# Two 64x64 levels of a block inverse in one matmul group, for two neighbouring chains of a gated delta rule

## The reference

```python
def step(S, x):
    qt, kt, vt, bt, gt = x
    S = S * jnp.exp(gt)[..., None, None]
    kv = jnp.einsum('bhk,ebhkv->ebhv', kt, S)
    delta = (vt[None] - kv) * bt[..., None]
    S = S + kt[None, :, :, :, None] * delta[..., None, :]
    ot = jnp.einsum('bhk,ebhkv->ebhv', qt * scale, S)
    return (S, ot)
```

## Time and profile before

| | |
|---|---|
| median of 3 runs | 3258.17 us |
| lowest and highest | 3254.01 and 3269.35 us |
| span of the profiled execution, which is its own time as the profile has it | 3278.8 us |
| mean granted TensorE clock | 0.943 |
| busy: PE, DVE, ACT, POOL | 91%, 51%, 34%, 45% of the span |
| last link of the chain of waits: PE, issue, DVE, ACT, POOL | 74%, 10%, 6%, 4%, 4% |
| the delta stage | about 1336 to 2008 us of the span |

### The profile page before, as it was taken

The page is one execution under the profiler, slowest core; times in us unless marked ns, Lnnn a source line. Parts: engine busy times, 40 slices in busy tenths (PEclk is TensorE's granted clock), DMA queues, the critical chain, the costliest instruction groups (busy, mean ns, idle before and its releaser), DMA issues.

```text
span 3278.8 us, 46022 instructions
## 1 busy us (share of the span) xinstructions
PE 2990.0 (91%) x16081; PEld 1719.2 (52%) x16081; DVE 1674.9 (51%) x3820; ACT 1128.2 (34%) x2501; POOL 1485.6 (45%) x1471
## 2 busy tenths in 40 slices
PE   7999999888999899679999998998999999999828
PEld 3434566577676544357777765444533333444414
DVE  7633266588244432258777632442257777621361
ACT  3312422297122222345666332221034444332201
POOL 0565656498554457333333103554656666300003
PEclk9999999999999899859999778999999999999958
DMA  5400001210111244334554435211167666600404
GB/s 169 138 19 6 13 19 54 68 43 14 42 51 43 69 159 158 125 97 123 135 132 124 123 112 162 83 52 49 30 203 201 205 198 198 160 13 26 175 4 129
DMA packets 275960, 321.36 MB, mean 98 GB/s; under 512 B 155807, under 2 KB 193569, under 8 KB 275732
## 3 DMA queue, kind: packets, MB, share of 16 engines
q1 hardware_dynamic: 219684, 182.57, 18.7%
q0 software_dynamic: 51840, 134.60, 13.6%
q10 hardware_dynamic: 4208, 1.25, 0.2%
HBM read 215.75 MB, written 104.60 MB: 98 GB/s over the span
## 4 chain that ended last, share of the span: by engine, by line
PE 74%; issue 10%; DVE 6%; ACT 4%; POOL 4%; DMA 1%; SPq 0%; ACTq 0%; DVEq 0%; POOLq 0%
PE bank L2700 8%; PE bank L1522 5%; PE bank L2692 5%; PE bank L708 4%; PE bank L1301 3%; PE bank L2363 3%; PE bank L2854 3%; PE bank L2847 3%; PE bank L439 3%; PE bank L731 2%; PE bank L762 2%; PE bank L1117 2%; PE bank L2343 2%; PE bank L1311 2%; PE bank L858 2%
## 5 line engine op out<-in xcount | busy, mean ns | idle before, releaser
L2672 POOL DMA_INDIRECT conv_src<-xn_rows,keep x288 | 272.4, 946 | 176.4 <-DVE conv_msg L2738 111.4
L291 POOL DMA_INDIRECT sorted_bias<-perf_rec,place x256 | 260.2, 1016 | 145.4 <-PE bank L708 90.1
L2700 PE MATMUL bank<-conv_msg,conv_hot 128*128 128x512 f32 x576 | 273.0, 596 | 0.6 <-ACT conv_msg L2719 0.6
L1923 POOL TENSOR_TENSOR delta_dec<-delta_dec,rates_of 128x512 f32<-128x512 f32 x64 | 67.3, 1051 | 338.4 <-ACT delta_dec L1975 338.4
L2738 DVE TENSOR_TENSOR conv_msg<-bank,conv_src 128x512 f32<-128x512 f32 x288 | 185.5, 686 | 47.3 <-PE bank L2692 47.3
L666 POOL DMA_INDIRECT sorted_edge<-rec,place x128 | 127.2, 994 | 141.0 <-PE bank L1362 75.1
L2719 ACT ACTIVATE conv_msg<-conv_msg 128x1024 f32<-128x1024 f32 x144 | 152.0, 1055 | 102.0 <-DVE conv_msg L2738 102.0
L1117 PE MATMUL bank<-bias_prod,bias_hot 128*128 128x256 f32 x640 | 148.2, 387 | 25.2 <-ACT bias_hot L1070 13.1
L2692 PE MATMUL bank<-conv_we,conv_eT 64*128 64x512 f32 x576 | 164.5, 648 | 0.7 <-ACT conv_eT L2716 0.7
L1101 POOL TENSOR_TENSOR bias_prod<-bias_col,bias_rec 128x512 f32<-128x512 f32 x128 | 147.2, 1179 | 16.5 <-PE bank L1117 15.7
L1117 PEld LDWEIGHTS bank<-bias_prod,bias_hot 128*128 128x128 f32 x640 | 120.1, 192 | 53.8 <-issue 28.2
(11 more groups left out here) (502 smaller groups left out, 6756.2 us busy)
## 6 DMA issues: line engine op xcount, KB each, us to landing
keep<-slot_qkv SPq DMA_DIRECT2D x32, 512.0 KB, 3.9
delta_kv<-slot_qkv SPq DMA_DIRECT2D x32, 512.0 KB, 3.9
sorted_edge<-sort_pad SPq DMA_DIRECT2D x8, 1440.0 KB, 7.3
keep<-sorted_edge SPq DMA_DIRECT2D x18, 640.0 KB, 5.2
slot_out<-delta_o SPq DMA_DIRECT2D x64, 128.0 KB, 2.0
conv_src<-xn_rows,keep POOLq DMA_INDIRECT x288, 3.6
X<-in_x SPq DMA_DIRECT2D x4, 1024.0 KB, 10.9
sorted_bias<-perf_rec,place POOLq DMA_INDIRECT x256
```

The lines of the kernel that those rows point to most:

```text
L291: POOL.indirect_dma_start(out=sorted_bias, out_offset=bass.IndirectOffsetOnAxis(ap=place[:, 0, c:c + 1], axis=0), in_=rec0[:, c, :], in_of ...
L2672: POOL.indirect_dma_start(out=src[:, n % 4, j, :], out_offset=None, in_=xn_rows, in_offset=bass.IndirectOffsetOnAxis(ap=rec[:, g % 3, k + ...
L2700: a = PE.matmul(bank[n % 2][:, :], hot[:, g % 2, k + j, :], msg[:, q, j, :], start=j == 0, stop=j == 1)
```

## The change

- The two steps Zb and T become one step, "Zb and T". For chain n it issues, head by head in turn, the Zb matmul of chain n and the T matmul of chain n - 1. One more such step, for n = NC, holds the last chain's T. It waits for U_ready of n, Zb_ready of n - 1 and T_ready of n - 2.
- `MID` goes from 16.2 to 15.8, and the fractions are set anew: Z .70, Z copy .80, U .05, U copy .15, Zb and T .21, Zb copy .25, T copy .26 (of the chain before), turn .65, kq .75, gram .22.
- Z waits for Z_ready of the chain before in place of T_ready, and U waits for U_ready of the chain before as well: each step waits for the readers of its own region of bank 3.

PE's order in a period is then: U .05, through .20, Zb and T .21, gram .22, decay .25, solve .55, turn .65, Z .70, sums .80. ACT's is: low mask .08, U copy .15, Zb copy .25, T copy .26, (L copy .33), exp .35, w .70, kq .75, Z copy .80.

```diff
--- before.py
+++ after.py
@@ -1701,7 +1701,7 @@
             BT = 4
             NBT = ST // BT
             NC = 2 * ST
-            MID, MAIN = 16.2, 17.2
+            MID, MAIN = 15.8, 17.2
             ALONE = 13
             gt = rates_of
             eg = sb("eg", [P, 3, ST, H])
@@ -1773,14 +1773,15 @@
 
             plan = []
             for n in range(NC):
-                for what, at in (("mask", -0.45), ("turn", -0.2), ("kq", -0.1), ("low mask", 0.08), ("gram", 0.21), ("decay", 0.25),
+                for what, at in (("mask", -0.45), ("turn", -0.35), ("kq", -0.25), ("low mask", 0.08), ("gram", 0.22), ("decay", 0.25),
                                  ("exp", 0.35), ("weigh", 0.45), ("BA", 0.72),
-                                 ("Z", MID + 0.005), ("Z copy", MID + 0.1), ("U", MID + 0.25), ("U copy", MID + 0.35),
-                                 ("Zb", MID + 0.5), ("Zb copy", MID + 0.6), ("T", MID + 0.75), ("T copy", MID + 0.85),
+                                 ("Z", MID - 0.1), ("Z copy", MID), ("U", MID + 0.25), ("U copy", MID + 0.35),
+                                 ("Zb and T", MID + 0.41), ("Zb copy", MID + 0.45), ("T copy", MID + 1.46),
                                  ("kd", MAIN - 0.3), ("through", MAIN), ("r", MAIN + 0.15), ("solve", MAIN + 0.35),
                                  ("w", MAIN + 0.5), ("sums", MAIN + 0.6), ("state", MAIN + 0.75), ("o", MAIN + 0.85),
                                  ("store", MAIN + 1.0)):
                     plan.append((n + at, what, n))
+            plan.append((NC + MID + 0.41, "Zb and T", NC))
             for t in range(ST):
                 plan.append((2 * t - 3.0, "load qk", t))
                 plan.append((2 * t + 1.8, "B out", t))
@@ -2014,7 +2015,30 @@
                                       stop=c == KC - 1)
                         if c == KC - 1:
                             a.then_inc(*gate_done.up())
-                    if what not in ("turn", "decay", "gram", "Z", "U", "Zb", "T", "through", "solve", "sums"):
+                    if what not in ("turn", "decay", "gram", "Z", "U", "Zb and T", "through", "solve", "sums"):
+                        continue
+                    if what == "Zb and T":
+                        if n < NC:
+                            PE.wait_ge(*U_ready.at(n + 1))
+                        if n >= 1:
+                            PE.wait_ge(*Zb_ready.at(n))
+                        if n >= 2:
+                            PE.wait_ge(*T_ready.at(n - 1))
+                        for i in range(HG):
+                            if n < NC:
+                                t, g, hs, MA, MB = places(n)
+                                h = g * HG + i
+                                a = PE.matmul(bank[3][64:128, 256 + 64 * i:320 + 64 * i], BA[0:64, t % R, h, 0, 64:128],
+                                              Lf[0:64, t % 2, h, :], start=True, stop=True)
+                                if i == HG - 1:
+                                    a.then_inc(*Zb_done.up())
+                            if n >= 1:
+                                t, g, hs, MA, MB = places(n - 1)
+                                h = g * HG + i
+                                a = PE.matmul(bank[3][0:64, 256 + 64 * i:320 + 64 * i], Zb[64:128, (n - 1) % 2, i, :],
+                                              U[64:128, t % 2, h, 64:128], start=True, stop=True)
+                                if i == HG - 1:
+                                    a.then_inc(*T_done.up())
                         continue
                     t, g, hs, MA, MB = places(n)
                     r, at = t % R, t % 2
@@ -2056,7 +2080,7 @@
                     if what == "Z":
                         PE.wait_ge(*ul_in[at].at(16 * 7 * (t // 2 + 1)))
                         if n >= 1:
-                            PE.wait_ge(*T_ready.at(n))
+                            PE.wait_ge(*Z_ready.at(n))
                         for i, h in enumerate(heads):
                             PE.matmul(bank[3][32:64, 32 * i:32 * i + 32], BA[0:32, r, h, 0, 32:64], Lf[0:32, at, h, 0:32],
                                       start=True, stop=True)
@@ -2065,6 +2089,8 @@
                         a.then_inc(*Z_done.up())
                     if what == "U":
                         PE.wait_ge(*Z_ready.at(n + 1))
+                        if n >= 1:
+                            PE.wait_ge(*U_ready.at(n))
                         for i, h in enumerate(heads):
                             PE.matmul(bank[3][0:32, 32 * i:32 * i + 32], Zs[32:64, n % 2, i, :], U[32:64, at, h, 32:64],
                                       start=True, stop=True)
@@ -2073,18 +2099,6 @@
                             a = PE.matmul(bank[3][32:64, P + 32 * i:P + 32 * i + 32], U[32:64, at, h, 32:64],
                                           Zs[32:64, n % 2, i, :], start=True, stop=True)
                         a.then_inc(*U_done.up())
-                    if what == "Zb":
-                        PE.wait_ge(*U_ready.at(n + 1))
-                        for i, h in enumerate(heads):
-                            a = PE.matmul(bank[3][64:128, 256 + 64 * i:320 + 64 * i], BA[0:64, r, h, 0, 64:128],
-                                          Lf[0:64, at, h, :], start=True, stop=True)
-                        a.then_inc(*Zb_done.up())
-                    if what == "T":
-                        PE.wait_ge(*Zb_ready.at(n + 1))
-                        for i, h in enumerate(heads):
-                            a = PE.matmul(bank[3][0:64, 256 + 64 * i:320 + 64 * i], Zb[64:128, n % 2, i, :],
-                                          U[64:128, at, h, 64:128], start=True, stop=True)
-                        a.then_inc(*T_done.up())
                     if what == "through":
                         if t >= 1:
                             PE.wait_ge(*state_new.at(n - 1))
```

## The result

The changed kernel takes 3248.56 us (median of 20 runs, 3238.56 to 3255.05), the kernel before 3258.68 us in the same session (20 runs, 3251.54 to 3280.86). The ratio is 0.9956 with a 95% interval of 0.9941 to 0.9972: 0.44% less, some 14 us (the two medians are 10 us apart), where 18 us were forecast. It was repeated twice beside other kernels: 0.9965 (0.9939 to 0.9991) and 0.9934 (0.9909 to 0.9959).

What follows compares the result with a forecast made beforehand. PE bounds one half of each batch, DVE the other. Five batches -10.3, load waits +2.1, last L copy period -1.15, tail -8.5, fill 0: -18 us, from 3258.17 to 3240 us, range 3220 to 3264.

Steps and rivals of the forecast that it cites:

- Part 1: Zb and T merged on PE: 16 alternating records take 0.60 us, saving 0.60 us of PE per chain.
- Part 2: PE-bound half: ACT's loop through the U copies sets a 7.49 us period against 7.79, gaining 0.30 per period.
- Part 3: Period with the L copy, once a batch: through of the next chain comes 1.15 us earlier.
- Part 4: First Z of a batch waits 0 to 0.9 us for loaded blocks, average 0.35; +2.1 us in all.
- Part 5: DVE-bound half of each batch: DVE's list is unchanged and has no idle time, so gain 0.
- rival C: DVE-bound half: longer waits before solve pull the granted clock down, some 30 us per stretch, 3270 or 3300; chance 0.13.
- Part 6: Fill and tail: fill 0; tail -8.5 us, from 16 chains saving 0.60 each and waits exchanged.
- rival D: Tail keeps full clock because PE's work is packed closer: up to 32 us more, 3210 to 3225; chance 0.07.
- Rival B: Merged pair does not overlap (1.07 to 1.20 us) or new waits eat the gain: -2 us, 3256; chance 0.17.
- Rival E: DVE ends every batch's half, so only tail and last L copy period count, less load waits: 3251; chance 0.08.

Runs made afterwards that it cites:

- e3: Changed kernel with Zb and T issued as two groups, all Zb first, at the same place; 3289.11 us, ratio to before 0.9975.
- e4: Changed kernel with the merged group placed behind gram instead of ahead of it; 3281.28 us, ratio to before 0.9951.
- e8: Changed kernel with the merged group behind gram and gram's matmuls issued twice for three chains of each batch; 3249.95 us, ratio to before 0.9968.
- e1: Kernel before, run again unchanged for a second profile; 3300.44 us, ratio to before 1.0018.
- e6: Kernel before without 29 of the 30 block columns of each batch on DVE; 3243.05 us, ratio to before 0.9947.
- e7: Changed kernel without 29 of the 30 block columns of each batch on DVE; 3211.03 us, ratio to before 0.9846.
- e5: Kernel before with six redundant 128x512 matmuls between the last decay and the first gate matmul; 3255.81 us, ratio to before 0.9986.
- e9: Changed kernel with the merged group behind gram and 20 of 30 block columns per batch moved to POOL; 3280.91 us, ratio to before 0.9945.
- e11: Same kernel as e9, run again beside the changed kernel; 3243.89 us, ratio to before 0.9910.

## Why the prediction was right and wrong

3248.56 us lies in the range (3220 to 3264), 8.6 us above the 3240 forecast. The change is 0.44%, short of the 0.5% line that the forecast had it just past; the interval (0.28 to 0.59%) takes in the line. That the number came out right is in part luck: in the profiles a term of -9 in the main part came out near 0, and one of -8.5 in the tail three to four times as large, and two such errors nearly cancel.

- **Part 1 (the merged group in 0.60 us): right.** 0.61. The bound of 1.20 for "no overlap" was wrong as well: e3 shows 0.90 for groups that are not interleaved.
- **Part 2 (ACT's loop, 7.49 us and 0.30 of wait): right in kind**, 7.35 to 7.42 and 0.21. What failed is the next sentence, "Gain per PE-bound period: 0.30", carried three times into each batch. DVE's rows at both ends of the light half, after and then before:

```profile
1639.54 0.85 DVE L2186 SCALAR_TENSOR_TENSOR delta_r<-bank,delta_eg,delta_kv 128x64 f32<-128x64 f32 x4
...
1666.16 1.29 DVE L2178 TENSOR_TENSOR delta_BA<-bank,delta_dec 128x512 f32<-128x512 f32 x2 [1.10 <-POOL delta_dec L1924]
```
```profile
1764.44 0.85 DVE L2172 SCALAR_TENSOR_TENSOR delta_r<-bank,delta_eg,delta_kv 128x64 f32<-128x64 f32 x4
...
1791.78 1.29 DVE L2164 TENSOR_TENSOR delta_BA<-bank,delta_dec 128x512 f32<-128x512 f32 x2 [1.77 <-POOL delta_dec L1923]
```

The half that DVE decides starts with BA. From r to BA it is 27.34 us before (1764.44 to 1791.78) and 26.62 after (1639.54 to 1666.16): 0.72 less. In its parts: to the first through -1.10; over the next two periods -0.14 (15.58 before, 15.44 after, with a wait of 0.89 of Z for the loads in them); from the third through to BA +0.52 (5.18 before, 5.70 from 1660.46 after). BA stands behind decay, exp and weigh, and the change puts the merged group and its wait (0.61 and 0.21) between through and decay, where only Z (0.37) stood. The gain was counted at through, and DVE starts from BA. This is read from one batch; no kernel with the merged group behind decay was run.
- **Part 3 (-1.15 once a batch): right**, -1.10 at through; half of it is given back at BA.
- **Part 4 (Z's waits for the loads, 2.1 us in all): low.** 3.9 us in six waits over the stage, the longest 1.3, since Z could start 10.4 to 11.9 us behind the L copy, about the 10.1 and 11.7 worked out; that the wait falls on all of them, not on half, makes the sum.
- **Part 5 (the DVE-bound half, 0): the step that failed.** At full clock its length is right (39.80 against 39.50), and "DVE has no idle time" nearly (38.53 busy of 39.80). But all that PE saves in it becomes a wait before solve: 2.7 us per 100 us before, 6.3 after (21.2 in 335). Three of the four half-clock stretches stand behind the longest of these waits, one a batch: one of 2.14 us ends at 1758.41, and from 1760.0 the clock is at 0.50 for 10.2 us. The fourth stands behind the 1.3 us wait of Z for the loads, and the other three long waits cost nothing. It is the long waits that go with it, not their sum: e4 has 25.5 us of them, none over 1.6, and 12 us at half clock. That the waits cause it is not shown, since e8 did not settle it; the table there has the odds. This is rival C, in stretches of 3 to 10 us and not of 70; I gave it 0.13. I held against it that waits of 1.3 us leave the clock at 1.00, by the rows of one batch. The trace of before has the counterexample: such a wait ends at 1617.93, and the clock is at 0.50 for 3.4 us from 1619.6. Over two profiles of before (382.5 and 380.9) and three of after (389.5, 377.8 and 382.8), the main part went from 381.7 to 383.4 on average, where -9.35 was forecast.
- **Part 6 (the tail, -8.5): its working holds, its condition did not.** Solve waits for the T copy 7 times, 6.0 us (forecast 7 times, 5.8), the sums for w 1.6 (1.1); a wait of 4.1 us of the first gate matmul for its input is not in before's first profile (it is 3.3 us in e1). The full-clock period in the tail is 6.87 us against 7.42. But the condition "if the half-clock stretch ends when it did" fell: the stretch is not there (rival D, chance 0.07).
- **Rival B** fell with the first row of the merged group. **Rival E** (DVE hides the batch gains, 3251, chance 0.08) is what e6 and e7 show for the main part: of up to 3.7 us a batch 1.6 at most are left in the batches at full clock (63.9 to 65.7, before 65.5). E's number is the nearest of all, but it too had the tail at -8.5.

So the cases were all named; I treated as exclusive what happened together, E and C in the main part and D in the tail. In short: the main part gained 0 to 2 us a batch at full clock and gave it back to the clock; the tail gained some 7 us by its shorter list, by the estimate at e5, and the rest by the clock.

**What stays open.** How long the tail's half-clock stretch is in a typical run of before: its two profiles lose 26 to 37 us of tail to after's, while the medians differ by 9 to 25 in all, and e5 gained 5. And why after's tail, which has no more work behind its last decay and a wait of 4.1 us, is back at full clock within 6.8 us where before stays down for 48 to 72. No run told that apart. Nor is it known why one wait of 2.1 us is followed by half clock and the next is not.

## What to carry to other kernels

In a loop with two regimes, count a saving at the instruction that starts the regime of the other engine, and look at what was put in front of it; a saving counted anywhere else may end there. Removing the suspected other bound from both kernels (e6 against e7) prices what it hides in one pair of runs. A saving that turns into waits need not be neutral: before taking idle time for free, look in the profile for the stretches at half clock and at what the engine did ahead of each. And where the clock has a part in it, one profile of each kernel is not enough: e9 and e11 are one kernel, and their main parts are 13 us apart.

## What the runs showed of the hardware

- Two groups of small matmuls issued one after the other overlap when they use different rows and columns of the array (e3): T's first record starts 0.29 us into Zb's 0.5, and 16 records take 0.90 us, 0.61 if they alternate.
- A DVE instruction on SBUF of 0.37 us takes 1.08 to 1.17 us beside a POOL product of 128x512 (e9).
- The granted clock is not a function of idle time alone: e5 holds 0.98 with 1000 records in 82.0 us and 6 us idle, before falls to 0.50 at 1848.3 with no wait over 0.65 us in the 13 us ahead of it, after falls for 6.8 us in a wait of 4.1 and recovers. Of 18 waits of 2.1 to 2.2 us, 9 are followed by a stretch at 0.50.
